# Selective-scan layer on one core: last stage rewritten, pieces transposed in pairs, variance sums of one column

## The reference, cut to what matters

```
proj = hidden @ in_proj_w.T                   # gate, x, B, C of each of 8 groups, and dt
xBC  = silu(causal convolution of 4 taps)
state = state * exp(dt*A) + dt*x*B ; y_t = state . C_t     # over 32 steps
y    = y + x * D
yn   = y * rsqrt(mean(y*y over 512 of a group) + 1e-5) * norm_weight * silu(gate)
x    = x + yn @ out_proj_w.T
```

```
x = x + where(query_sel & row_sel, conv(x) @ W.T + bias, 0)
```

## Time and profile before

| | us |
|---|---|
| median of 3 runs | 1660.18 |
| the profiled execution's own time | 1662.89 |
| its span, first to last instruction | 1661.1 |
| tensor engine (PE) busy | 1619.4 |
| DVE, ACT, POOL busy | 1066.9, 857.0, 780.9 |

### The profile page before, as it was taken

How to read it: one execution, slowest core, us unless ns; L and a number is a source line. 1 busy time by engine, 2 the same in 40 slices (tenths; PEclk the granted TensorE clock), 3 DMA queues, 4 the chain that set the end, 5 groups by cost and what they waited for, 6 DMA issues and landing times.

```text
span 1661.1 us, 31702 instructions
## 1 busy us (share of the span) xinstructions
PE 1619.4 (97%) x12495; PEld 1300.1 (78%) x12495; DVE 1066.9 (64%) x1772; ACT 857.0 (52%) x1378; POOL 780.9 (47%) x766
## 2 busy tenths in 40 slices
PE   9999999999999999999999999999999999998997
PEld 6678888888888888877778888888888888886665
DVE  6967666566656566777676656665656666564456
ACT  4654546555555555455554555555555545554221
POOL 4464645545463636444254554546364645544103
PEclk9999999999999999999999999999999999999999
DMA  6110102011111111020112201111011102016772
GB/s 202 35 58 29 43 20 64 27 52 39 46 45 33 58 34 43 16 64 26 33 39 71 65 27 52 39 41 50 33 58 33 39 20 65 27 35 148 167 164 102
DMA packets 50291, 93.09 MB, mean 56 GB/s; under 512 B 5664, under 2 KB 6304, under 8 KB 50144
## 3 DMA queue, kind: packets, MB, share of 16 engines
q1 hardware_dynamic: 50144, 91.06, 19.0%
HBM read 82.59 MB, written 8.45 MB: 55 GB/s over the span
## 4 chain that ended last, share of the span: by engine, by line
PE 81%; issue 7%; ACT 4%; POOL 4%; DVE 3%; POOLq 0%; DVEq 0%
PE PS L478 47%; PE PS L744 19%; PE PS L592 3%; PE PS L1084 2%; PE PS L1030 2%; PE PS L650 2%; PE PS L711 2%; ACT big L533 1%; PE PS L357 1%; PE PS L602 1%; PE PS L570 1%; DVE cb L513 1%; POOL yl L704 1%; PE PS L571 1%; PE PS L206 1%
## 5 line engine op out<-in xcount | busy, mean ns | idle before, releaser
L478 PE MATMUL PS<-xh,wh 128*128 128x512 f32 x1280 | 529.7, 414 | 0.6 <-DVE xl L367 0.6
L478 PE MATMUL PS<-xh,wl 128*128 128x512 f32 x1280 | 503.2, 393 | 0.0
L478 PE MATMUL PS<-xl,wh 128*128 128x512 f32 x1280 | 500.3, 391 | 0.0
L513 DVE SCALAR_TENSOR_TENSOR cb<-PS,P,cb 128x496 f32<-128x496 f32 (+2 forms) x576 | 412.6, 716 | 98.4 <-ACT cb L499 82.7
L182 POOL TENSOR_TENSOR wl<-rw,wh 128x512 fp32r<-128x512 f32 x160 | 207.4, 1299 | 183.6 <-ACT wh L177 165.2
L478 PEld LDWEIGHTS PS<-xh,wl 128*128 128x128 f32 x1280 | 240.5, 188 | 55.9
L478 PEld LDWEIGHTS PS<-xh,wh 128*128 128x128 f32 x1280 | 241.1, 188 | 46.2 <-ACT wh L177 1.0
L478 PEld LDWEIGHTS PS<-xl,wh 128*128 128x128 f32 x1280 | 241.9, 189 | 43.1
L698 POOL TENSOR_TENSOR ysum<-yq 128x256 f32<-128x256 f32 x128 | 95.5, 746 | 375.4 <-ACT yq L686 375.4
L499 ACT ACTIVATE cb<-PS,P 128x512 f32<-128x512 f32 x192 | 149.2, 777 | 221.2 <-PE PS L478 220.9
L744 PE MATMUL PS<-oh,yh 128*128 128x512 f32 x512 | 203.0, 396 | 6.4 <-POOL yl L704 5.4
(11 more groups left out here) (193 smaller groups left out, 2238.1 us busy)
## 6 DMA issues: line engine op xcount, KB each, us to landing
rw<-in_w_in SPq DMA_DIRECT2D x160, 256.0 KB, 2.7
ro<-in_w_out SPq DMA_DIRECT2D x64, 256.0 KB, 2.9
wh<-x2s SPq DMA_DIRECT2D x32, 258.5 KB, 5.0
wl<-x2s SPq DMA_DIRECT2D x32, 258.5 KB, 5.2
x2s<-acc SPq DMA_DIRECT2D x16, 260.0 KB, 4.0
out_x<-acc SPq DMA_DIRECT2D x16, 256.0 KB, 2.3
acc<-in_x SPq DMA_DIRECT2D x3, 1024.0 KB, 9.6
acc<-in_x SPq DMA_DIRECT2D x4, 256.0 KB, 4.1
```

What stands on the lines that cost most here:

```text
L478: fn = lambda e, k=k, w=w, v=v, i=i: e.matmul(PS[:, bank, :], w[:, m, 128 * k:128 * k + 128], v[:, k, a:a + 512], start=(i == 0), stop=(i ...
L513: dve.op(lambda e, d=d, w=w: e.scalar_tensor_tensor(out=cv[:, :, d:32], in0=pv[:, :, 0:32 - d], scalar=w, in1=cv[:, :, d:32], op0=ALU.mult ...
```

## The change

What it does:

- Transposes in pairs. A(n, 0) and A(n, 1) both stand in slot 7, A(n, 2) and A(n, 3) both in slot 9, ahead of Y(n, 0). The four tiles now use banks `TB` = 2, 5, 2, 7. So the readers of these banks' earlier contents and the next writers have new waits: Y(n, 0) waits for `A_dve(n, 1)`, and O(n, 0), which writes bank 7, waits for `A_dve(n, 3)`. `A_dve(n, 1)` moves to slot 8.
- One-column variance sums. `S` multiplies by one column of ones and not by 128, and tiles 1 and 2 share one group (`sums`); `rstd` and the power act on the pair. `add_out` of tile 1 moves from slot 4 to slot 5. `yss` gets a place for each tile, in free space of `big`.
- The rest of stage 31 is written out in `last_products`: the first convolution `second(0)` goes ahead of everything that is left, the reads of y ahead of the variance work, O(31, 1) gets bank 4, and the four sums are two pairs.

```diff
+        TB = (PT, PO[2], PT, PO[0])
+        def sums(n):
+            return ((0,), (1, 2), (3,)) if n < NS - 1 else ((0, 1), (2, 3))
...
         def A(n, i):
-            z, a = 4 * n + i, 128 * i
+            a = 128 * i
...
-            if z >= 1:
-                pe.wait("dtx", divmod(z - 1, 4))
-            if z == 0:
-                pe.wait("alo", 0)
+            if i == 0:
+                for m in range(6):
+                    pe.wait("silu", (n, m))
+                if n >= 1:
+                    pe.wait("dtx", (n - 1, 2))
+                else:
+                    pe.wait("alo", 0)
+            elif i == 1:
+                pe.wait(*(("acc", (n - 1, 2)) if n >= 1 else ("xl", 7)))
+            elif i == 2:
+                pe.wait("dtx", (n, 0))
+            else:
+                pe.wait("L", (n, 0))
             for j in range(4):
-                fn = lambda e, j=j: e.transpose(PS[:, PT, 128 * j:128 * j + 128], xs[:, j, a:a + 128], ident)
+                fn = lambda e, j=j: e.transpose(PS[:, TB[i], 128 * j:128 * j + 128], xs[:, j, a:a + 128], ident)
...
-        def S(n, i):
...
-            pe.op(lambda e: e.matmul(PS[:, PG, 256 + 128 * r:384 + 128 * r], yss[:, r, :], C[:, C_ONE:C_ONE + 128],
-                                     start=True, stop=True), "S", (n, i))
+        def S(n, tiles):
...
+            for i in tiles:
+                fn = lambda e, i=i: e.matmul(PS[:, PG, 256 + i:257 + i], yss[:, i, :], C[:, C_ONE:C_ONE + 1], start=True, stop=True)
...
         def O(n, i):
...
             if i == 0:
-                pe.wait("L", (n, 0))
+                pe.wait("dtx", (n, 3))
             elif i == 1:
-                pe.wait("acc", (n, 0))
+                pe.wait(*(("acc", (n, 0)) if n < NS - 1 else ("ev", (n, 7))))
...
+        def last_products():
+            n = end_n
+            second(0)
+            y_dve(n, 0)
+            y_act(n, 0)
+            y_pool(n, 0)
+            for i in (2, 3):
+                A_dve(n, i)
+                M_dve(n, i)
+                if i == 2:
+                    y_dve(n, 1)
+            y_act(n, 1)
+            weights2(0)
+            y_pool(n, 1)
+            for i in (2, 3):
+                y_dve(n, i)
+                y_act(n, i)
+                y_pool(n, i)
+            for k in (1, 2, 3):
+                weights2(k)
+            O(n, 0)
+            Y(n, 2)
+            Y(n, 3)
+            O(n, 1)
+            S(n, (0, 1))
+            O(n, 2)
+            O(n, 3)
+            S(n, (2, 3))
+            for tiles in sums(n):
+                rstd(n, tiles)
+                for i in tiles:
+                    add_out(n, i)
```

More of the change, by code:

```diff
@@ L455, in adaln_attn_ffn_kernel, with summed @@
         shared = [("mx", 3)]
+        def sums(n):
+            return ((0,), (1, 2), (3,)) if n < NS - 1 else ((0, 1), (2, 3))
+        def summed(n, i):
+            return next(g[-1] for g in sums(n) if i in g)
         def who(n):
@@ L642, in Y @@
                 pe.wait("L", (n, 1))
+                pe.wait("dtx", (n, 1))
                 if n >= 1:
@@ new lines, in rstd @@
+        def rstd(n, tiles):
+            a, b, last = tiles[0], tiles[-1] + 1, (n, tiles[-1])
+            dve.wait("S", last)
+            if n >= 1:
+                dve.wait("rs", (n - 1, summed(n - 1, tiles[-1])))
+            dve.op(lambda e: e.tensor_scalar(vr[:, a:b], PS[:, PG, 256 + a:256 + b], 1.0 / 512.0, 1e-5, ALU.mult, ALU.add), "var", last)
+            pool.wait("var", last)
+            pool.wait("mh", 0)
+            if n >= 1:
+                pool.wait("acc", (n - 1, tiles[-1]))
+            pool.op(lambda e: e.tensor_tensor(rs[:, a:b], vr[:, a:b], bc(mh[:, 0:1], 128, b - a), ALU.pow), "rs", last)
@@ L803, in stage @@
         def stage(n):
-            real, prev = n < NS, n >= 1
+            prev = n >= 1
             b = block_at.get(n)
@@ L807, in stage @@
                 chain.extend(D_chain(0))
-            for m in range(10 if real else 7):
+            for m in range(10):
                 lag = 1
@@ L895, in stage @@
                         Y(n - 1, 3)
-                if real and m == 2:
+                if m == 2:
                     G_all(n)
@@ L902, in stage @@
                         O(n - 1, i)
-                        S(n - 1, i)
-                if real:
-                    if m == 7:
-                        seg(n)
-                        expo(n)
-                    if m >= 7:
-                        A(n, m - 7)
-                    if m == 9:
-                        Y(n, 0)
-                        Y(n, 1)
-                if prev and m == 0:
-                    A(n - 1, 3)
-                if n == NS:
-                    if m == 4:
-                        one_hot()
-                    if m <= 3:
-                        weights2(m)
-                    if m >= 2:
-                        second(m - 2)
+                        for tiles in sums(n - 1):
+                            if tiles[-1] == i:
+                                S(n - 1, tiles)
+                if m == 7:
+                    seg(n)
+                    expo(n)
+                    A(n, 0)
+                    A(n, 1)
+                if m == 9:
+                    A(n, 2)
+                    A(n, 3)
+                    Y(n, 0)
+                    Y(n, 1)
         end_n = NS - 1
```

130 lines of the change are left out of this document (59 added, 71 removed).

## The result

| | before | changed |
|---|---|---|
| median of the runs side by side, us | 1661.24 (4 runs, 1657.32 to 1663.25) | 1754.37 (4 runs, 1749.66 to 1757.25) |
| profiled execution's own time | 1662.89 | 1757.25 |
| its span | 1661.1 | 1755.3 |
| mean granted clock of the span | 0.991 | 0.978 |

The ratio is 1.056, with a 95% interval of 1.0527 to 1.0595. The forecast was 1761 us, in a range of 1722 to 1785, and slower with 0.95.

What follows compares the result with a forecast made beforehand. In the 32 stages PE's own list was taken as the bound. 76 + 32 + 0 - 7 = 101 us on the profiled 1662.9 gave 1764, and 1761 as median, 2.7 lower; range 1722 to 1785.

Steps and rivals of the forecast that it cites:

- The added wait, 31 x 2.45 = 76 us: O(n, 0) waits for `A_dve(n, 3)` 2.45 us in each of 31 places, 76 us.
- The clock, 32 us: PE's clock falls to half after two in three of the new waits, 1.5 us each, 32 us lost.
- One-column sums, 0: A variance sum on PE costs two weight loads, 0.22 us, whatever its columns; nothing saved.
- rival of cheap sums: The variance sums' loads hide and up to 28 us go; 1733 to 1745 us, chance 0.05.
- Transposes in pairs, 0: On PE, eight transposes in a row cost two groups of four, about 0.44 us each; nothing saved.
- The other bound, 6 us for the pairs: If 0.09 us were paid at each change of kind on PE, 64 pairs of transposes would save 6 us.
- Nothing given back: PE's 0.34 us wait ahead of the products of B and C stays, so no added wait is recovered.
- `add_out` of tile 1 in slot 5, under cover: This addition hides under a 2.8 us projection and an evacuation; without cover, piece 5's taps late by under 1 us a stage.
- The last stage, 7 us saved: Rest of stage 31: waits and slow clock of 10.8 us shrink, saving 7 us, between 3 and 11.
- no fall of the clock: Rival: PE's clock holds after the new waits; 1729 us, chance 0.15.
- Longer falls than one stretch: Rival: two half-clock stretches after each new wait; 162 us more, 1822 us, chance 0.05.
- A met wait: Rival: DVE finishes `A_dve(n, 3)` before O(n, 0) is reached, so the kernel is faster; 1653 us, chance 0.04.

Runs made afterwards that it cites:

- e2: Changed kernel with DVE's order changed: `dtx` of tile 3 ahead of the taps of piece 0; 1657.95 us, ratio 0.9970 to the kernel before.
- e5: Changed kernel with ScalarE's `x3_act` of tile 0 moved behind the read-outs' casts in the last stage; 1748.65 us, ratio 1.0520 to the kernel before.
- e3: Kernel before with one-column sums alone; 1657.43 us, ratio 0.9970.
- e8: Changed kernel with the fourth tile's transposes put back and sums as two-column bf16 matmuls; 1638.50 us, ratio 0.9871 to the kernel before.
- e4: Changed kernel with 22 unread matmuls filling the wait ahead of the first output product; 1732.45 us, ratio 1.0421 to the kernel before.
- e10: Changed kernel with 11 unread matmuls ahead of the first output product, filling half the wait; 1736.96 us, ratio 1.0453 to the kernel before.

## Why the prediction was right

The mechanism was right: the wait, what causes it, and the clock behind part of the waits. That the first term came out to the microsecond is in part luck, since two errors in it cancel.

- **The added wait, 31 x 2.45 = 76 us.** The stages are 2.45 us longer, 76.0 in all. But a wait costs 2.68 (e2), 83 us in all. The working took the lateness of `dtx` in the trace of before, 1.95, plus 0.44 for the four transposes, plus 0.06 for the signal. This gives how late the product starts, and that is 2.59 and not 2.45: from the end of `dtx` to the start it is 0.15 us (1041.58 to 1041.73). The first product then holds the next one 0.08 longer, which no term had. The idle time of 2.43 beside it is counted from the modelled end of the matmul before and is not the same quantity. What held is the chain that sets `dtx`'s time (projection, evacuation, taps, y, yg): from the start of projection 0's last matmul to the end of `dtx` it is 5.39 us in a middle stage of both kernels. The wait was taken to be some tenths shorter in the three stages with mixing work; they are 2.55, 2.43 and 2.64.
- **The clock, 32 us.** 18 of 31 fell, at 1.55 us each: 27.9. The share of two in three was a choice between two neighbours and came out near; that is luck, as no row before could size it, and e5 has 17 of 31. That the price of one fall is 1.5 holds. Unforeseen was that half-clock stretches elsewhere changed too, 3 us to the good. The mixing layer's waits, too, have a fall behind them in some of the traces and none in others.
- **One-column sums, 0.** The distance is the same in e3, from the 64-column row. The rival of cheap sums fell, and so did the 8 us that the Trainium skill's issue gap would have given ("TensorE: Matmul & The Clock Gate", section "Back-to-back issue gap"): 0.45 us with one column and with 128. But e3's 2 to 3 us of quicker projections behind the sum are not in the forecast. And the working, two loads of 0.11 make the 0.22, is not what the rows show: from a one-column sum to the projection is 0.14 us, and the other 0.09 is the projection's slower first distance (0.31 against 0.23), which e8 keeps.
- **Transposes in pairs, 0.** This step failed, by little: "Four transposes at 0.11 each fill the 0.44 without it, so I take nothing." Up to the second matmul behind the group it holds: 1.1 us for eight and 0.67 for four; less one pace of 0.23, that is 0.87 and 0.44. But the projection behind the group stays slower beyond that point (e2), and the pairs and the one-column sums together save 0.23 us a stage, 7 us, of which e3's sums alone are 2 to 3. The other bound, 6 us for the pairs, was the nearer one. These 7 us hide the 7 by which the wait was taken too small.
- **Nothing given back.** The wait ahead of the products of B and C is still 0.34 us (8.2 us for 24 of them).
- **`add_out` of tile 1 in slot 5, under cover.** Nearly: PE waits twice for it, 0.7 us each, in the two stages in which the decay's inputs are made (L443). The prediction had not named this reader; 1.4 us.
- **The last stage, 7 us saved; measured 4.7.** The step that failed is "O(31, 0) waits for the last `dtx`. Before, that ended at 1523.20 + 0.68 = 1523.9 [...] it ends near 1523.2. That is a wait of 3.0 us". The wait is 5.37. The convolution was counted as cover on PE only. It also issues a step on ACT, `x3_act(0)`, and that stands ahead of the square of y in ACT's list and waits for the convolution's end. e5 moves it and has 3.15, the figure of the prediction nearly.

The sum: 76 + 32 - 7 = 101 forecast; measured 83 for the waits, 27.9 for the clock, and given back 7 by pairs and one-column sums, 3.0 by half-clock stretches elsewhere and 4.7 in the last stage. That is 96; less the 1.6 of the start, which is no effect of the change, 94.6, where the spans differ by 94.2.

The rivals: no fall of the clock was e4's kernel, 1732 (1729 forecast for it). Longer falls than one stretch did not come behind the 2.43 us. A met wait is e2, where DVE takes `dtx` before the taps: then the kernel is 0.3% faster, 1658, where that rival had 1653.

## What to carry to other kernels

When a bank or buffer gets a second user, look up in the trace of before when its last reader ends, and compare with the start of the new writer; that one difference, times the stages, was most of the 94 us here. Where a wait comes out as forecast, look also at what the rest of the stage did: here it had become shorter, and the wait cost more than its idle time. When a step is moved ahead, follow it into every engine's list: the step that cost 2 us of the last stage's gain was one activation that came along with the convolution. And the releaser that a trace names for a wait on several semaphores is worth a look at when it ended.

## What was not expected of the hardware

- Waits alike to the hundredth, at the same place of alike stages, are followed by a half-clock stretch or not: 18 of 31 at 2.43 us, 3 of 31 at 1.25 us (e10), none behind work (e4). What decides in the single case is left open here.
- A float32 matmul of one column takes PE as long as one of 128, 0.45 us to the second matmul behind it; a bf16 one with two columns 0.35, and a second one behind it only some 0.03 more.
- A short group costs beyond its neighbour: the projection behind four transposes takes 2.62 us from its first to its last matmul start, behind a one-column sum 2.60 (e3), and 2.49 with nothing ahead of it.
